# A transformer layer with routed experts: key moves split by group, a power on GpSimd, weight loads behind gathers, a last block in halves

## What is computed

```python
x = L0_attn_hidden_states                       # (8, 256, 256)
x = x + attn(layernorm(x))                      # rope, causal softmax, 32 heads on 8 key/value heads of 64
x = x + ffn(layernorm(x))                       # below

gate_logits = x @ gate_kernel                   # (..., 8)
top_k_weights = softmax(top_2(gate_logits))
h0, h1 = x @ w0[e], x @ w1[e]                   # 256 -> 512, for the two experts e of a row
out = sum over both of weight * ((silu(h0) * h1) @ wo[e])
```

## Time and profile before

| | us |
|---|---|
| median of 3 runs | 798.24 |
| lowest, highest | 796.76, 799.06 |
| the profiled execution | 795.58 |
| its span (first to last instruction) | 793.8 |
| TensorE busy | 747.8 (94%) |
| VectorE busy | 560.9 (71%) |
| ScalarE busy | 505.5 (64%) |
| GpSimd busy | 428.3 (54%) |

### The profile page before, as it was taken

How to read it: one execution, slowest core, us unless ns; L and a number is a source line. 1 busy time by engine, 2 the same in 40 slices (tenths; PEclk the granted TensorE clock), 3 DMA queues, 4 the chain that set the end, 5 groups by cost and what they waited for, 6 DMA issues and landing times.

```text
span 793.8 us, 19659 instructions
## 1 busy us (share of the span) xinstructions
PE 747.8 (94%) x6080; PEld 640.4 (81%) x6080; DVE 560.9 (71%) x2166; ACT 505.5 (64%) x1562; POOL 428.3 (54%) x673
## 2 busy tenths in 40 slices
PE   5799999999999999999999999999799999999993
PEld 5678888888888888888888888877577777888883
DVE  6887677667666757766775785888756656777772
ACT  2678877776776777677777667768554433555551
POOL 1466665656656556465565546555424544566552
PEclk9899999999999999999999999999999999999997
DMA  8343031212211211221221212123973232222330
GB/s 251 97 125 117 29 89 48 68 41 68 74 35 55 61 62 47 63 67 39 71 68 35 61 41 68 41 67 109 374 266 51 43 53 41 50 42 48 55 54 5
DMA packets 52854, 61.07 MB, mean 77 GB/s; under 512 B 10544, under 2 KB 45616, under 8 KB 52752
## 3 DMA queue, kind: packets, MB, share of 16 engines
q1 hardware_dynamic: 44816, 50.07, 20.6%
q0 software_dynamic: 7488, 9.36, 7.0%
q10 hardware_dynamic: 448, 0.39, 0.3%
HBM read 26.21 MB, written 9.32 MB: 45 GB/s over the span
## 4 chain that ended last, share of the span: by engine, by line
PE 72%; DVE 13%; issue 5%; DMA 4%; ACT 4%; POOL 1%; SPq 1%; POOLq 0%; DVEq 0%; ACTq 0%
PE h L1669 12%; PE attn_out L541 10%; PE projected L387 9%; PE probsT L501 9%; PE scores L488 8%; PE heads_out L520 5%; PE yb L1711 4%; PE projected L408 3%; PE heads_out L523 2%; PE yb L1694 2%; PE projected L365 2%; PE tg L1682 2%; DMA xs<-xn_rows,from_token 2%; DVE masked L759 1%; DVE masked L761 1%
## 5 line engine op out<-in xcount | busy, mean ns | idle before, releaser
L1011 POOL TENSOR_SCALAR probs<-exps,inv_sums 128x128 f32<-128x128 f32 x256 | 96.5, 377 | 215.2 <-DVE inv_sums L767 165.0
L626 ACT COPY pT<-probsT 128x384 f32<-128x384 f32 x256 | 121.7, 475 | 79.2 <-PE probsT L501 79.1
L617 ACT ACTIVATE exps<-masked,neg_max 128x128 f32<-128x128 f32 x256 | 103.1, 403 | 57.8 <-DVE neg_max L761 57.4
L501 PE MATMUL probsT<-identity,probs 128*128 128x128 f32 x768 | 130.2, 279 | 5.3 <-ACT pT L626 5.2
L619 ACT ACTIVATE exps<-masked,neg_max 128x256 f32<-128x256 f32 x256 | 127.3, 497 | 0.0
L1012 POOL TENSOR_SCALAR probs<-exps,inv_sums 128x256 f32<-128x256 f32 x256 | 124.7, 487 | 0.0
L1972 POOL DMA_INDIRECT out<-y,to_token x39 | 69.3, 1777 | 94.7 <-DVE y L1888 48.9
L387 PE MATMUL projected<-xT_hi,w 128*128 128x256 f32 x488 | 106.4, 298 | 2.5 <-DVE k_sin L749 1.6
L1669 PE MATMUL h<-experts_w,xsT_hi 128*128 x312 | 104.6, 416 | 4.0 <-DVE experts_w L1559 2.0
L488 PE MATMUL scores<-kT,qT 64*128 64x128 f32 (+1 forms) x1024 | 103.1, 340 | 5.6 <-DMA qT<-rotated 4.1
L761 DVE CUSTOM_DVE_ANT_0 masked<-scores,tables 128x256 f32<-128x256 f32 x256 | 107.5, 420 | 0.2 <-issue 0.2
(11 more groups left out here) (208 smaller groups left out, 1683.1 us busy)
## 6 DMA issues: line engine op xcount, KB each, us to landing
qT<-rotated SPq DMA_DIRECT2D x254, 64.0 KB, 2.2
experts_w<-w_in SPq DMA_DIRECT2D x16, 512.0 KB, 7.6
kT<-k_cos SPq DMA_DIRECT2D x62, 128.0 KB, 3.4
raw<-w_attn SPq DMA_DIRECT2D x20, 256.0 KB, 3.0
experts_w_out<-w_out SPq DMA_DIRECT2D x8, 512.0 KB, 9.1
out<-x_all SPq DMA_DIRECT2D x8, 256.0 KB, 2.4
xn_rows<-raw SPq DMA_DIRECT2D x8, 256.0 KB, 2.7
x_all<-x SPq DMA_DIRECT2D x1, 1792.0 KB, 11.2
```

The source lines that it names most:

```text
L501: mm = nc.tensor.transpose(p_bank[:, at:at + P], probs[:, h, at:at + P], ident[:, :])
L617: nc.scalar.activation(exps[:, h, 0:P], masked[:, h, 0:P], ACT.Exp, bias=neg_max[:, h, 0:1], scale=-1.0, accum_out=sums[:, h, 0:1])
L626: nc.scalar.copy(pT[:, n % 2, h, :], p_bank[:, 0:3 * P]).then_inc(pT_done, 1)
L1011: nc.gpsimd.tensor_scalar(probs[:, h, 0:P], exps[:, h, 0:P], inv_sums[:, h, 0:1], 1.0, ALU.mult, ALU.mult)
```

## The change

Keys of half 0 of batch 0 are moved group by group, each with a semaphore of its own, in 16 DMAs of 32 KB in place of four of 128 KB; the query moves of turns 0 and 1 stand between. The inverse deviations of attention's normalisation are made by one GpSimd instruction (a power of -0.5) in place of VectorE's Newton steps. Statistics of nine of the 14 later tiles, taken before turn 0, move into turns 0 and 1. Loads of expert slots 3 to 7 and w_out 2 to 7 each wait for the landing of a certain gather. In batch 7 one layer normalisation's moments and first Newton step move one slot on; ScalarE's table load for silu moves behind the last copy of attention; in block 1 the residual stands ahead of the gating of block 0. The last two blocks use plain float32 for the output, and h1, gating, transposes, copies and output of the last block are done in halves, in banks of their own.

```diff
+    def move_first_keys(q, group, a):
+        for copy in range(2):
+            at = copy * HD + a * 32
+            q.dma_start(kT[at:at + 32, 0, group, :], k_cos[group:P:HALF, a, :]).then_inc(first_keys_in[group], 16)
...
-            if g == 7:
-                sp.wait_ge(s_ps, (TURNS - 1) * GROUP)
-                rt["load_slot"](sp, 3)
-                sp.wait_ge(r["out_started"], 16 * LAST)
-                sp.wait_ge(r["xn2_done"], LAST)
-                for i in (4, 5, 6):
-                    rt["load_w_out"](sp, i)
...
         sp.wait_ge(k_rotated, 1)
-        for copy in range(2):
-            at = copy * HD
-            sp.dma_start(kT[at:at + 32, 0, :, :], k_cos[:, 0, :]).then_inc(k_in[0], 16)
+        move_first_keys(sp, 0, 0)
         sp.wait_ge(q_rotated, 1)
         for a in range(2):
             sp.dma_start(qT[a * 32:a * 32 + 32, 0, :, :], rotated[0:P:2, 0, a, :]).then_inc(q_in[0], 16)
+        for a in range(2):
+            move_first_keys(sp, 1, a)
         move_q(1, 1, True)
+        for group in range(2, HALF):
+            for a in range(2):
+                move_first_keys(sp, group, a)
         for i in range(SLOTS + 2, SLOTS + EARLY):
             load_piece(i)
         batches(turn)
+        def gathered(block):
+            sp.wait_ge(r["xs_in"][block % RING], 16 * (block // RING + 1))
         sp.wait_ge(exp_done, TURNS * GROUP)
+        sp.wait_ge(s_ps, TURNS * GROUP)
+        sp.wait_ge(r["out_started"], 16 * LAST)
+        sp.wait_ge(r["xn2_done"], LAST)
+        gathered(0)
+        gathered(1)
+        gathered(2)
+        rt["load_slot"](sp, 3)
         rt["load_w_out"](sp, 2)
-        rt["load_w_out"](sp, 3)
         sp.wait_ge(pT_ps, TURNS * GROUP)
-        rt["load_slot"](sp, 4)
         sp.wait_ge(o_ps, TURNS)
-        rt["load_slot"](sp, 5)
         sp.wait_ge(y_ps, BATCH)
-        rt["load_slot"](sp, 6)
         sp.wait_ge(y_added, BATCH)
         sp.dma_start(t["out"][LAST]...)
+        gathered(3)
+        rt["load_slot"](sp, 4)
         rt["store_last_rows"](sp)
+        rt["load_w_out"](sp, 3)
+        gathered(4)
+        rt["load_w_out"](sp, 4)
+        rt["load_slot"](sp, 5)
+        gathered(5)
+        rt["load_w_out"](sp, 5)
+        rt["load_slot"](sp, 6)
+        gathered(6)
+        rt["load_w_out"](sp, 6)
+        sp.wait_ge(r["out_last"], 16)
         rt["load_slot"](sp, 7)
-        sp.wait_ge(r["out_last"], 16)
+        gathered(7)
         rt["load_w_out"](sp, 7)
...
-        keep_busy(9)
+        keep_busy(6)
...
             maxima(b, g, 0)
+            if (b, g) == (0, 1):
+                tile_stats(TT + 8, TT + 11)
...
-            if b == 0 and g == 0:
+            if (b, g) == (0, 0):
+                tile_stats(TT + 5, TT + 8)
+            if (b, g) == (0, 1):
+                wait_own(tile_stats(TT + 11, TILES))
                 moments_start(TT, TILES)
-            if b == 0 and g in (1, 2):
-                newton_steps(TT, TILES, {1: 0, 2: 2}[g], {1: 2, 2: 3}[g])
+            if (b, g) == (0, 2):
+                dve.wait_ge(rstd_done, 2)
...
-            if (g, slot) == (2, 2):
+            if (g, slot) == (2, 3):
                 rt["row_moments"](dve, LAST - 1)
-            if (g, slot) == (2, 3):
+            if (g, slot) == (3, 0):
                 rt["row_newton"](dve, 0, 1)
...
+        def inverse_deviations(n, a, b):
+            pool.wait_ge(variance_done, n + 1)
+            nc.gpsimd.tensor_tensor(rstd[:, a:b], newton[:, 0, a:b], newton[:, 1, a:b], ALU.pow).then_inc(rstd_done, 1)
...
+        def last_block_ends(expert):
+            for half in range(2):
+                ...                      # h1, half of the columns, into its own bank
+            pe.wait_ge(gT_done, LAST)
+            for half in range(2):
+                pe.wait_ge(gated_done, LAST + 1 + half)
+                ...                      # two transposes
+            for half in range(2):
+                pe.wait_ge(gT_done, LAST + 1 + half)
+                ...                      # two of the four plain products with w_out
...
-        def last_transposes():
-            g_transposes(LAST)
-
-        output_parts(LAST - 1, last_transposes)
-        output(LAST, expert)
+        last, expert = expert, following
+        g_transposes(LAST - 1)
+        pe.wait_ge(xT_lo_done, LAST + 1)
+        slots_ready(LAST)
+        hidden(LAST, expert, 0, nothing)
+        output(LAST - 1, last)
+        last_block_ends(expert)
...
+        x_lo(1)
         gate_rows(0)
-        x_lo(1)
```

More of the change, by code:

```diff
@@ L172, in attention @@
     k_in = r["k_in"] = [sem("k_in0"), sem("k_in1")]
+    first_keys_in = [sem(f"first_keys{g}_in") for g in range(HALF)]
     s_ps = sem("s_ps")
@@ L742, in rope_k @@
             dve.wait_ge(k_ps, 2 * b + half + 1)
-            if half == 1:
-                dve.wait_ge(k_in[0], b * 64 + 64)
+            if half == 1 and b == 0:
+                for group in range(HALF):
+                    dve.wait_ge(first_keys_in[group], 64)
+            elif half == 1:
+                dve.wait_ge(k_in[0], b * 64)
             elif b > 0:
@@ L927, in routing_last, with tile_stats @@
                 rt["lane_codes"](dve, 0, 1, 1)
+        def tile_stats(a, b):
+            for i in range(a, b):
+                ins = nc.vector.bn_stats(stats[:, i, :], x_all[:, i, :])
+            return ins
         def moments_start(a, b):
@@ L932, in moments_start @@
             wait_own(ins)
[L934 to L946, removed]
+            nc.vector.tensor_scalar(newton[:, 0, a:b], moments[:, a:b, 1], EPS, None, ALU.add).then_inc(variance_done, 1)
         dve.wait_ge(x_first_in, 16)
@@ L965, in vector @@
         dve.wait_ge(x_rest_in, 16)
-        for i in range(TT, TT + 3):
-            nc.vector.bn_stats(stats[:, i, :], x_all[:, i, :])
+        tile_stats(TT, TT + 3)
         rope_q(1, False, o_bank)
         split_w(3)
[L970 to L974, removed]
+        tile_stats(TT + 3, TT + 5)
         split_w(4)
@@ L1614, in experts @@
     r["rank_bank"], r["pair_bank"] = bank("ranks"), bank("pairs")
-    xs_in = [sem(f"xs_in{p}") for p in range(RING)]
+    xs_in = r["xs_in"] = [sem(f"xs_in{p}") for p in range(RING)]
     xT_ps = sem("xsT_ps")
@@ L1713, in output_parts @@
                     n += 1
+            mm.then_inc(yb_ps, 1)
+        def last_block_ends(expert):
+            for half in range(2):
+                n = 0
+                for k in range(KT):
+                    for x, part in ((xT_hi, 0), (xT_hi, 1), (xT_lo, 0)):
+                        at = expert * 2 * WI + part * WI + (KT + k) * MLP + half * MLP // 2
+                        mm = nc.tensor.matmul(last_h1[half][:, 0:MLP // 2], x[:, LAST % RING, k * P:(k + 1) * P],
+                                              w[:, bass.ds(at, MLP // 2)], start=(n == 0), stop=(n == 3 * KT - 1))
+                        n += 1
+                mm.then_inc(h1_ps, 1)
+            pe.wait_ge(gT_done, LAST)
+            for half in range(2):
+                pe.wait_ge(gated_done, LAST + 1 + half)
+                for k in range(MT // 2):
+                    at = half * MLP // 2 + k * P
+                    mm = nc.tensor.transpose(last_tg[half][:, k * P:(k + 1) * P], gated[:, at:at + P], ident[:, :])
+                mm.then_inc(gT_ps, 1)
+            for half in range(2):
+                pe.wait_ge(gT_done, LAST + 1 + half)
+                for k in range(half * MT // 2, (half + 1) * MT // 2):
+                    mm = nc.tensor.matmul(last_yb[:, 0:EMB], gT_of(LAST)[:, k * P:(k + 1) * P],
+                                          w_out[:, bass.ds(expert * WO + k * EMB, EMB)],
+                                          start=(k == 0), stop=(k == MT - 1))
             mm.then_inc(yb_ps, 1)
@@ L1741, in tensor @@
         following = owner(1)
-        for j in range(1, BLOCKS):
+        for j in range(1, LAST):
             last, expert = expert, following
@@ L1762, in tensor @@
             hidden(j, expert, 1, next_addresses)
-            if j < LAST:
-                x_transposes(j + 1)
+            x_transposes(j + 1)
             outputs_ready(j - 1)
-            if j < LAST:
-                output(j - 1, last)
+            output(j - 1, last)
             if j == EARLY_BLOCKS - 1:
@@ L1802, in g_copy, with g_copy_half @@
                 return
-            nc.scalar.copy(gT, tg[:, :]).then_inc(gT_done, 1)
+            nc.scalar.copy(gT_of(j), tg[:, :]).then_inc(gT_done, 1)
+        def g_copy_half(half):
+            act.wait_ge(gT_ps, LAST + 1 + half)
+            nc.scalar.copy(gT_of(LAST)[:, half_columns(half)], last_tg[half][:, 0:MLP // 2]).then_inc(gT_done, 1)
         def second_split_hi(j):
@@ L1830, in scalar @@
         x_copy(0)
-        for j in range(BLOCKS):
+        for j in range(LAST):
             if j == 2:
@@ L1853, in gate_rows, with gate_last_rows @@
             nc.vector.tensor_tensor(gated, h1[:, :], act_h, ALU.mult).then_inc(gated_done, 1)
+        def gate_last_rows():
```

(7 more changed lines are left out.)

69 lines of the change are left out of this document (43 added, 26 removed).

## The result

The changed kernel takes 806.38 us (median of six runs, 803.55 to 806.97), the one before 797.50 in the six runs beside them: ratio 1.0115, 95% interval 1.0096 to 1.0135. It is slower by 9 us. The prediction said 799.2, within 793.5 and 803.0.

The account below looks back on a forecast made before the run. The prediction took TensorE as the bound (72% of the chain), with idle time at the stages' ends. Terms 3.3 - 1.3 - 1.3 + 1.5 - 1.2 = +1.0 us gave 799.2 on the median of 798.24, range 793.5 to 803.0.

Parts of the forecast that it names:

- Start: First turns: eight new key moves on SyncE delay the load of piece 6 and so TensorE, +3.3 us (2.7 to 5).
- the 1.1 us that the second rotation was to come earlier: Start: rotation of the second query group at 16.4 in place of 17.52, taken off the key moves' 4.4 us.
- Power and statistics: Start and first turns: GpSimd power replaces VectorE steps, rows 1 us earlier but worth nothing; spread statistics net 0.
- Batch 7: Moments moved behind the rotation that the first ranks wait for, so the 1.5 us wait goes: -1.3 us (0 to -1.5).
- Seam: Between attention and experts: paced loads, moved table load and residual together give -1.3 us (-0.1 to -1.7).
- The part of the term that was for the moved steps: Seam: later table load worth 0.7 us, residual of block 1 ahead of the gating worth 0.5.
- pacing, put at 0.1: Seam: paced loads let the first gather land 2.7 us earlier, only about 0.1 of it on the path.
- Blocks: Expert blocks 1 to 8: paced loads now meet gathers and scatters, +1.5 us (0 to +3.5).
- two collisions at half their price: Blocks: half a collision of 2.7 us taken twice, 2.7, less a slack of 1.2.
- paced loads take the gathers' turn: Rival, slower: collisions at blocks 4 to 8 cost 3.5 us, key moves 0.64 each; +4.5, 802.7 us; chance 0.23.
- a term near 0: Blocks under packet-wise sharing: a gather waits for a packet, not the backlog; 797.7 us, about a third of the forecast's chance.
- Tail: Last block in halves: split-weight wait of 2.4 us gone, then the chain of scatters limits; -1.2 us (-0.8 to -2.4).

Follow-up runs that it names:

- keys_late: Changed kernel with the eight key moves of groups 2 and 3 issued behind the loads of pieces 6, 7 and 8: 798.13 us, ratio 1.0004 to the kernel before.
- unpaced: Changed kernel with the expert loads issued as in the kernel before, each as its memory comes free: 800.48 us, ratio 1.0040 to the kernel before.
- held: Changed kernel, expert loads respread: none before the third gather, then 5 MB without gathers, then at most 512 KB per landing: 803.10 us, ratio 1.0089 to the kernel before.
- power_only: Kernel before with only the power on GpSimd, the spread statistics and the shorter warm-up: 798.00 us, ratio 1.0011.
- tail_only: Kernel before with only the change to the last two blocks: 794.81 us, ratio 0.9972.
- piece6_first: Kernel before with the loads of pieces 6 and 7 ahead of the four moves of the second query group: 796.12 us, ratio 0.9990.
- steps7: Kernel before with only batch 7's moments and first Newton step one slot later; one execution, batch 7 to last query move 0.34 us shorter.
- both_undone: Changed kernel with key moves of groups 2 and 3 behind the load of piece 8 and expert loads as before: 795.22 us, ratio 0.9983 to the kernel before.
- best3: both_undone with loads of pieces 6 and 7 ahead of the second query group's moves, pieces 9 to 13 ahead of later query moves: 791.43 us, ratio 0.9937.
- busy9: Changed kernel with nine identity products of warm-up in place of six: 804.93 us, ratio 1.0095 to the kernel before.
- best1: Changed kernel, pieces 6 and 7 loaded ahead of second query group's moves, key groups 2 and 3 behind piece 8, expert loads as in held: 794.56 us, ratio 0.9972.
- best2: best3 with expert loads from slot 3 and w_out 2 on held until the first gather has landed, then in one stream: 791.62 us, ratio 0.9945.

## Why the prediction was wrong, step by step

**Start, +3.3 (2.7 to 5), measured +6.1.** The mechanism held: the load of piece 6 stands behind eight moves, and its delay of 6.2 us is passed on to TensorE nearly whole (5.95). Two terms were mis-sized. The eight moves took 5.92 us in place of 4.4: each 0.59 to 0.60 plus 0.04, and one of them 1.41. Of the two ends, 0.43 and 0.60, I took the middle; the row of moves into the same tile was the right one. At 0.64 each, with the spacing, the term would have been 4.0; the long issue is the rest of what the moves took. The Trainium skill ("DMA: Bandwidth & Descriptors", section "Rules for kernel authors") says that under 64 KB one pays mostly overhead. The trace agrees: 32 KB cost the queue what 128 KB do. The other term, the 1.1 us that the second rotation was to come earlier, wasn't there. I counted it from the landing of x; but in before the product ahead of that rotation waits for TensorE, not for statistics, as its timeline says:

```profile
17.52 0.69 DVE L737 TENSOR_TENSOR by_cos<-heads_out,tables 128x512 f32<-128x512 f32 x1 [0.79 <-PE heads_out L387]
```

The bracket names the releaser, and I had read the start time only. In after that projection began 0.96 earlier and, at the lower clock, took 2.94 in place of 1.70, so the product began at 17.79, 0.27 later. At the upper level the gain wasn't there either: in keys_late, unpaced, held and power_only, with the clock at 1.00, the normalised rows came 1.1 to 1.3 us earlier than in before, but the projection began at 15.77 to 15.90, as in before (15.79). What held it there was not taken apart.

**Power and statistics, 0.** Right in size: no difference shown alone. The power took 0.72 us on two columns, and the normalised rows came 1.2 us earlier (5.75 against 6.98), near the 1 that I took.

**Batch 7, -1.3, measured -0.2 (alone -0.3).** The step that failed is that the wait's length was counted as gain. It went, but TensorE, 1.5 us earlier, was stopped soon after by a copy of ScalarE (0.26) and the next rotation of VectorE (0.59), whose total work had not changed.

**Seam, -1.3 (-0.1 to -1.7), measured -0.4.** Between the last query move and the first scatter, the five traces with the loads as in before and the rest of the seam unchanged (before, tail_only, piece6_first, steps7, power_only) give 0, 0.9, 0, 0.9 and 1.7 against before, the three unpaced ones with the seam's steps moved (unpaced, both_undone, best3) 1.5, 0.5 and 0.5, and the five paced ones (after, keys_late, busy9, held, best1) all -0.3 to -0.4. So pacing is worth about 1 us here on the mean (0.8 against -0.3), and before's trace lay at the good end. The moved table load and residual show nothing: 0.8 with them, 0.7 without. The wait of 1.4 for the residual is gone, but the gating that now stands behind it is waited for in its place, as the list of after's waits says:

```profile
PE h L1715 <- DVE raw L1931: 1.1, 1, 1.1
```

The part of the term that was for the moved steps, 1.2 of the 1.3, was wrong, and pacing, put at 0.1, was the part that paid.

**Blocks, +1.5 (0 to +3.5), measured +7.2.** The term was mis-sized, and with it the sum. I had seen the mechanism (a crowded gather, 2.7 us more, two collisions at half their price) and judged that each group would be nearly through when the next gather runs. Four things were not in it. The group of 1.5 MB issued from 606.57 on had landed by 614.82, 8.2 us later, and the next gather went out at 613.26. Scatters are crowded as well (5.3 and 7.4 us), and GpSimd's order puts the next gather behind the scatter. The clock fell behind the longest wait and cost 1.6 us more. And, as I read the order of the issues (no run takes it apart), the release feeds on itself: the later a gather lands, the nearer its loads are to the next one. The rival "paced loads take the gathers' turn" was the right case, with half its price. The Trainium skill ("DMA: Bandwidth & Descriptors", section "Queues, rings and completion order") has each DMA engine go round its queues packet by packet. By that a gather would pay little for a backlog; here gathers beside 1.5 MB took 6.5 and 7.4 us, against 2.7 to 4.1 for those of before from block 4 on, so the measurement decides against a term near 0.

**Tail, -1.2 (-0.8 to -2.4), measured -1.8, alone -2.1.** Right, but for the last scatter, which waits for VectorE's scaling and not for the landing before it. The last three scatters of after:

```profile
789.25 1.57 POOL L2060 DMA_INDIRECT out<-y,to_token  x1 [3.22 <-DMA out<-y,to_token]
792.83 1.55 POOL L2060 DMA_INDIRECT out<-y,to_token  x1 [2.01 <-DMA out<-y,to_token]
796.50 1.55 POOL L2060 DMA_INDIRECT out<-y,to_token  x1 [2.11 <-DVE y L1975]
```

They start 3.6 and 3.7 us apart, where I had 4.0 and 4.2 and before 4.8 and 4.7.

Together: 2.8 too little at the start, 1.1 and 0.9 too much gain in batch 7 and at the seam, 5.7 too little in the blocks, 0.6 too little gain in the tail make 9.9, the distance between +1.0 and +10.9.

Not settled: what lowers the clock at the start in some executions, and what makes the blocks cost 4.4 us in one execution and 7.2 in another under the same loads, which may also be why the times of keys_late spread over 6 us.

## What to carry to other kernels

On an in-order queue, look at what stands *behind* the issues that an edit adds: eight small moves that nobody was waiting for cost 6 us because one load stood behind them, and behind that load, in keys_late, the start was within the 1 to 1.5 us by which starts differ anyway. Loads released by the landing of a gather ran beside the next one here; let them run where none is due, or in one early stream, which cost about 1 us at the seam. Removing a wait gains its length only if the releaser of the next wait comes earlier too; read the releaser in the brackets, not the order of the start times.

## What the runs showed of the hardware

An SBUF-to-SBUF move mostly costs its queue 0.58 to 0.60 us at 32 KB, as at 128 KB, and now and then one issue takes 1.3 to 2.2 us. A gather of 128 rows lands mostly in 2.7 to 3.5 us where no load group runs, and in up to 7.6 beside 1.5 MB of loads (keys_late); a scatter mostly in 2.7 to 4.6, and in up to 7.5 beside such a group (8.0 in best2). Behind a wait of 4 us TensorE's next eight output products took 3.03 and 3.22 us (after, keys_late) in place of 1.9. GpSimd's power takes 0.72 us on two columns and 2.60 on 14.
